# Gated cross-attention with a mixture of experts: probabilities times values in groups of four chunks

## The reference, cut to what matters

```python
# x: 32 x 56 x 256, context: 32 x 1500 x 256, 16 heads of 16
q = layernorm(x) @ Wq.T + bq
k = context @ Wk.T + bk
v = context @ Wv.T + bv
scores = clip(q k / 4, -50, 50), masked positions at -50
probs = softmax(scores)
delta = layernorm(residual_scale * ((probs v) @ Wo.T + bo)) * gamma + beta
x = x + tanh(g_xattn) * delta
# then 8 experts, the best two of each token, h = relu(y w_fc)^2, out = h w_proj
x = x + tanh(g_ffn) * experts(layernorm(x))
```

## Time and profile before

| | |
|---|---|
| median of 3 runs | 1268.37 us (1267.36 to 1270.18) |
| the profiled execution | 1267.26 us, its span 1265.1 us |
| TensorE busy | 1248.7 us, 99% of the span |
| VectorE busy | 964.8 us, 76% |
| ScalarE busy | 688.5 us, 54% |
| GpSimd busy | 174.6 us, 14% |
| chain that ended last | TensorE 94%; `sc_ps` L412 23%, `o_ps` L427 14% |

### The profile page before, as it was taken

One profiled execution on the slowest core, in us unless ns is written; L12 is line 12 of the kernel. 1 busy time (PEld: TensorE's weight loads), 2 busy tenths in 40 slices (PEclk: granted clock), 3 DMA queues, 4 the chain that ended last, 5 costly groups with the idle time before them and its releaser, 6 DMA issues.

```text
span 1265.1 us, 51469 instructions
## 1 busy us (share of the span) xinstructions
PE 1248.7 (99%) x22040; PEld 1129.9 (89%) x22040; DVE 964.8 (76%) x1806; ACT 688.5 (54%) x854; POOL 174.6 (14%) x142
## 2 busy tenths in 40 slices
PE   7999999999999999999999999999999999899998
PEld 6888888888888888888888888888888888899998
DVE  6678777878787877787777878787878777687555
ACT  5555555556555556565555555565555565344443
POOL 1000101010101010010001010101010100154443
PEclk9999999999999999999999999999999999899999
DMA  5121212121112112121211121211121120010000
GB/s 158 52 67 43 64 53 70 53 66 56 55 51 68 55 42 71 47 70 53 70 50 57 53 70 53 67 55 54 51 69 55 45 74 5 19 64 10 17 8 17
DMA packets 29507, 68.19 MB, mean 54 GB/s; under 512 B 6037, under 2 KB 13458, under 8 KB 29330
## 3 DMA queue, kind: packets, MB, share of 16 engines
q1 hardware_dynamic: 20450, 54.61, 14.2%
q10 hardware_dynamic: 8880, 10.75, 2.6%
HBM read 60.77 MB, written 3.67 MB: 51 GB/s over the span
## 4 chain that ended last, share of the span: by engine, by line
PE 94%; issue 2%; DVE 1%; POOL 1%; ACT 0%; DMA 0%; DVEq 0%; POOLq 0%; ACTq 0%
PE sc_ps L412 23%; PE o_ps L427 14%; PE k_ps L369 10%; PE v_ps L370 7%; PE v_ps L369 7%; PE v_ps L371 7%; PE k_ps L371 7%; PE k_ps L370 7%; PE sc_ps L369 3%; PE sc_ps L370 3%; PE sc_ps L371 3%; PE k_ps L444 1%; POOL h_lo L352 1%; PE k_ps L457 1%; DVE h_sq L1043 0%
## 5 line engine op out<-in xcount | busy, mean ns | idle before, releaser
L610 ACT ACTIVATE prob<-sc_ps,m_bias 125x896 f32<-125x896 f32 x384 | 366.3, 1005 | 321.8 <-PE sc_ps L412 321.8
L915 DVE TENSOR_SCALAR prob<-prob 125x896 f32<-125x896 f32 x384 | 245.1, 642 | 140.8 <-ACT prob L610 137.4
L412 PE MATMUL sc_ps<-q_hi,kh 64*125 64x224 f32 x1536 | 228.5, 294 | 0.0
L370 PE MATMUL v_ps<-wv_lo,c_hi 128*125 128x256 f32 x764 | 214.8, 281 | 0.0
L369 PE MATMUL v_ps<-wv_hi,c_hi 128*125 128x256 f32 x764 | 214.3, 280 | 0.0
L371 PE MATMUL v_ps<-wv_hi,c_lo 128*125 128x256 f32 x764 | 214.0, 280 | 0.0
L412 PE MATMUL sc_ps<-q_hi,kl 64*125 64x224 f32 x1536 | 209.8, 270 | 0.0
L412 PE MATMUL sc_ps<-q_lo,kh 64*125 64x224 f32 x1536 | 209.3, 269 | 0.0
L427 PE MATMUL o_ps<-prob,vst 125*17 125x56 f32 x12288 | 189.2, 214 | 0.0
L427 PEld LDWEIGHTS o_ps<-prob,vst 125*17 125x17 f32 x12288 | 158.3, 98 | 31.5 <-issue 9.8
L763 DVE SCALAR_TENSOR_TENSOR kl<-k_ps,cst,kh 128x500 fp32r<-128x500 f32 x192 | 141.5, 738 | 46.5 <-ACT kh L597 44.7
(11 more groups left out here) (129 smaller groups left out, 1913.7 us busy)
## 6 DMA issues: line engine op xcount, KB each, us to landing
raw<-in_ctxT SPq DMA_DIRECT2D x96, 500.0 KB, 3.5
w_raw<-in_we ACTq DMA_DIRECT2D x16, 256.0 KB, 3.7
xq<-in_x ACTq DMA_DIRECT2D x16, 112.0 KB, 2.0
xr<-in_x ACTq DMA_DIRECT2D x16, 112.0 KB, 3.6
x_scratch<-x ACTq DMA_DIRECT2D x16, 112.0 KB, 3.7
out_y<-acc SPq DMA_DIRECT2D x7, 256.0 KB, 2.0
acc<-x_scratch SPq DMA_DIRECT2D x1, 1280.0 KB, 6.3
rec<-rec SPq DMA_DIRECT2D x64, 14.0 KB, 2.3
```

Source lines behind the costliest of these rows:

```text
L370: pe.matmul(ps, w_h, m_l, start=False, stop=False)
L412: last = pe.matmul(sc_ps[0:TC, 2 * (c % 2) + r, m * HS * S:(m + 1) * HS * S], k[rows, g % 2, m, cs], q[rows, b, m, :, :], start=term == 0, ...
L610: act.activation(prob[0:TC, c % PB, :].rearrange("p (c n) -> p c n", c=2), sc_ps[0:TC, 2 * (c % 2):2 * (c % 2) + 2, 0:NH * S // 2], ACT.Ex ...
L915: dve.tensor_scalar(p, p, EXP_LO, EXP_HI, ALU.max, ALU.min).then_inc(clip_done, 1)
```

## The change

`pv` leaves its place at the end of every unit. It now stands behind the second `scores` of every even unit, ahead of the projections, and takes four chunks there: in unit u the chunks 2u-4 to 2u-1, and in unit 0 the last four of the pair before. Odd units have none. Its waits are made once per four chunks. The ring of probability buffers grows from four to six. Behind the last pair four chunks are left over in place of two.

```diff
-PB = 4
+PB = 6
...
             def pv(i, c):
...
-                if c % 2 == 0:
-                    pe.wait_ge(v_evac, i * UN + c // 2 + 1)
-                    pe.wait_ge(clip_done, n + 2)
+                if c % GC == 0:
+                    pe.wait_ge(v_evac, i * UN + c // 2 + 2)
+                    pe.wait_ge(clip_done, n + GC)
...
                     scores(i, 2 * u + 1)
+                    if half == 0 and not (first and u == 0):
+                        if first and u == 2:
+                            pe.wait_ge(o_clear, 1)
+                        for d in range(GC, 0, -1):
+                            pv(*((i, 2 * u - d) if u > 0 else (i - 1, PC - d)))
                     if more:
                         k_proj(n, half, (q + 1) % 2, freed.get(u))
...
-                    if first and u == 1:
-                        pe.wait_ge(o_clear, 1)
-                    if not (first and u == 0):
-                        for d in (2, 1):
-                            pv(*((i, 2 * u - d) if u > 0 else (i - 1, PC - d)))
...
-            for d in (2, 1):
+            for d in range(GC, 0, -1):
                 pv(NP - 1, PC - d)
```

## The result

The changed kernel takes 1285.19 us in the median of 4 runs (1282.88 to 1287.43), against 1267.86 us (1267.19 to 1270.18, 4 runs) before: a ratio of 1.0133 with a 95% interval of 1.0108 to 1.0158. It is slower by 17 us. The forecast had the sign and the main term, but 1276.3 us, and its range ended at 1284. The profiled execution took 1282.88 us, 15.6 more than that of before, and is the fastest of the four. All ratios in this document leave out two far slower executions, one of 6710 us of the kernel before and one of 2376 us of the fourth experiment.

A forecast was written before the change was run, and what follows sets the result against it. TensorE, busy 99%, was taken to set the time. Seam waits of 19.4 us less 11.5 from merging gave +7.9: profiled 1267.26 to 1275.2 us, and with the median 1.1 above, 1276.3 us; range 1266 to 1284.

The forecast's parts named there:

- the sign: Whole kernel: the change makes it slower, by +7.9 us; slower by over 0.2% was given 0.72.
- the main term: Scores of unit 10: a wait of about 1.1 us that outweighs the merging; chance 0.62.
- What bounds the kernel: In the pairs TensorE, busy 99% of the span, sets the time; VectorE is next at 76%.
- the merging: Four-chunk `pv` between scores and keys: 1.70 us against 1.82 for two two-chunk ones, 0.12 gained per merge, 11.5 us.
- The rival in which each change of shape costs the same: TensorE's shape changes: 96 fewer at 0.16 us each gain 15.4 us, giving 1272.4 us; chance 0.13.
- the one in which the sides of the run cost nothing: Scores to `pv` and `pv` to keys: up to 0.41 us gained per merge, half likelier, 1262.8 us; chance 0.12.
- The seam of unit 10: Unit 9's values to unit 10's scores: TensorE waits 1.11 us for VectorE's `kl`, in 15 pairs, 16.7 us.
- The small seams: Waits before other even units: 0.08 us behind unit 1, 15 times, 1.2 us; first and last pair together 1.5 us.
- The ring: Six probability buffers in place of four: costed at nothing, since chunk c needs `pv` of c - 6, done a unit earlier.
- The long burst runs dry: Rival, in the 128 `pv` starts: second half at half speed, 96 x 0.78 = 75 us, 1351 us; chance 0.03.
- The sum: Whole kernel: 19.4 us lost at seams less 11.5 gained by merging, +7.9 us.

The follow-up runs named there:

- the fourth experiment: The changed kernel with its four-chunk `pv` at the end of odd units, of the group's own chunks, and four buffers: 1288.13 us, ratio 1.0153.

## Why the prediction was wrong

- **What bounds the kernel, and the merging:** right. A four-chunk run costs 1.70 us between scores and keys, with 0.20 ahead of it and 0.14 behind: the gain is 0.12 per merge, 11.5 us in 96. The rival in which each change of shape costs the same, and the one in which the sides of the run cost nothing, are out: two units without side step come to 10.65 us once the wait is taken off, where the forecast had 10.64 and equal changes would give 10.60.
- **The seam of unit 10:** right in place and cause, and nearly in size: 1.04 us measured for 1.11 forecast, in 14 pairs and not 15, since the last pair's VectorE has less to do; 14.5 us for 16.7. The experiment that moves `x_after` took 11 us of it away. The small seams: unit 1 of the middle pairs does not wait (1.2 us forecast); the first and last pair have seven waits, 2.0 us where 1.5 were forecast. All seams together cost 16.6 us, not 19.4.
- **The ring:** right, at nothing.
- **The step that failed** is the rival "The long burst runs dry", given 0.03 and argued away with "The even 0.77 us of the first 64 speaks against it". The 64 only show that what is already fetched can be taken at 12 ns; they say nothing on how much is fetched. The numbers to ask were on the page, the instruction queue's packets and bytes. Its price was wrong too: the run does not slow down to half, it stops now and then for 0.3 to 2.4 us, 9.3 us in all in the profiled execution with the hole ahead of the keys. It should have stood in the sum, as a cost from nothing up to one fetch per run, and the range should have reached further up.
- **The sum as measured**, on the profiled executions: 14.5 for unit 10, 2.0 for the first and last pair, -11.5 for the merging, 9.3 for the holes: +14.3 of the +15.6 us. Of the rest, 0.9 us lies ahead of the first scores, where the two kernels have the same order (they start at 17.64 in place of 16.75 us). Without the holes the sum is +5 where the forecast had +7.9, so the seam was put too dear by 2.8 us, and this hid a part of what was missing: the number came nearer than the mechanism deserved. The other three executions of the changed kernel took 1 to 5 us longer than the profiled one. They were not traced; that their holes are more or longer is likely, since the number differs from trace to trace, and was not shown.

## What to carry to other kernels

When short instructions are gathered into one run, ask for the run's length in instructions as well as in time, and compare it with what one fetch of the instruction queue brings. Here a run of 192 instructions was as good as free, one of 256 failed in a tenth of the cases, those in which the border of a packet fell late in it, and one of 512 in all. And before a piece of work of the bounding engine is moved, look at which late result of another engine it covers: here the two chunks at the end of the odd units covered VectorE's longest run of work, so the kernel that kept a run at each such place and merged the rest gained what the change had meant to.

## What the runs showed of the hardware

TensorE's products start 12 ns apart (1.56 us for 128), but its instructions come in packets of 16 KB, 256 each, and when its instructions go faster than packets come TensorE stops at the border, for up to 3.3 us and with no semaphore involved; the profile calls it "issue". From the start of the awaited packet to the end of the hole are 2.3 to 2.9 us in the nine runs, and a run of 128 takes its 256 instructions in 1.56. The two longest holes of the changed kernel, 2.4 and 1.9 us from start to start, fall into stretches of heavy traffic, as the windows (PEclk, DMA share and GB/s last) just ahead of the first of them and of an undisturbed unit show:

```profile
411.00:415.00 4.00, 3.16 (x143) 2.92 (x143) 3.05 (x7) 2.94 (x3) 0.48 (x1) 1.00 0.80 228
...
594.00:597.00 3.00, 3.00 (x135) 2.78 (x137) 2.27 (x6) 2.21 (x3) 0.00 (x0) 1.00 0.09 20
```

The packets that ended these two holes took 1.1 us, no longer than others, but they started 1.4 and 1.0 us behind the start of the run, where those of the other seven started between 1.1 us ahead of it and 0.1 behind. That the context and weight loads hold the start of the instruction packets back is my reading; no run took the loads away.
